# A four-image convolution, attention and top-k expert kernel: image 0's opening rewritten, and expert masks built on ScalarE

## The reference, cut to what matters

```python
# block 1, per image
x_ln = layernorm(x, ln_g, ln_b)
q = x_ln @ wq + bq                                   # read as an image of 128 channels
o = gelu(depthwise_conv_7x7_stride2(q_img) + dw_b)   # 8x8 positions
offsets = conv_1x1(o)
interp = grid_sample_bilinear_zeros(x, tanh(offsets) + refs)
k, v = interp @ wv + bv                              # 64 keys
att = softmax(qh @ kh.T) @ vh                        # 8 heads
z = att @ mo_w + mo_b + x
t = gelu(layernorm(z) @ mlp_w + mlp_b) + z
# block 2
t = t + landmark_attention(ln(t))                    # 4 best of 16 segments per head
# block 3
q = layernorm(ln(t) @ Wq.T + bq)                     # 8 heads
sc0, ix0 = top_k(l2norm(q[:half]) . l2norm(keys0), 16);  sc1, ix1 = the same for the other half
fs, pos = top_k(all sums sc0 + sc1, 16);  fi = ix0 + ix1 at pos
w = softmax(fs)
out = sum over the 16 of gelu(t . expert_down[fi]) * w * expert_up[fi]
t = t + out
```

## Time and profile before

| | us |
|---|---|
| median of 3 runs | 451.5 |
| lowest and highest | 449.02, 451.69 |
| the profiled execution, device time | 449.87 |
| its span, first to last instruction | 447.8 |
| mean granted TensorE clock | 0.701 |

### The profile page before, as it was taken

The page is one execution under the profiler, slowest core; times in us unless marked ns, Lnnn a source line. Parts: engine busy times, 40 slices in busy tenths (PEclk is TensorE's granted clock), DMA queues, the critical chain, the costliest instruction groups (busy, mean ns, idle before and its releaser), DMA issues.

```text
span 447.8 us, 7841 instructions
## 1 busy us (share of the span) xinstructions
PE 308.1 (69%) x2275; PEld 225.2 (50%) x2275; DVE 358.4 (80%) x2163; ACT 140.7 (31%) x324; POOL 217.9 (49%) x411
## 2 busy tenths in 40 slices
...
DMA packets 1634, 3.50 MB, mean 8 GB/s; under 512 B 180, under 2 KB 1205, under 8 KB 1592
## 3 DMA queue, kind: packets, MB, share of 16 engines
...
## 4 chain that ended last, share of the span: by engine, by line
DVE 55%; PE 23%; POOL 9%; issue 6%; ACT 6%; DMA 1%; DVEq 0%; ACTq 0%; POOLq 0%
PE bank L876 6%; DVE Sx L1363 5%; DVE i L1369 5%; DVE i L1370 5%; DVE cands L1419 4%; DVE onehot L494 4%; DVE vraw L1366 3%; DVE vraw L1360 3%; DVE segmax L1244 3%; DVE c L1416 3%; PE bank L540 2%; PE bank L550 2%; DVE masked L1426 2%; PE bank L783 2%; ACT hat L914 2%
## 5 line engine op out<-in xcount | busy, mean ns | idle before, releaser
L876 PEld LDWEIGHTS bank<-weights,onehot 108*128 108x128 f16 x1024 | 69.0, 178 | 3.1 <-DVE onehot L494 1.5
L876 PE MATMUL bank<-weights,onehot 108*128 108x16 f16 x1024 | 69.0, 216 | 1.9 <-DVE onehot L494 1.4
L1644 POOL TENSOR_TENSOR inv<-nrm,mhalf 128x16 f32<-128x16 f32 x8 | 23.4, 2925 | 35.8 <-DVE nrm L1376 35.8
L458 POOL TENSOR_TENSOR taps<-qpad,wa 128x128 f32<-128x128 f32 x96 | 36.0, 427 | 2.0 <-ACT qpad L929 1.9
L540 PE MATMUL bank<-wa,hat 128*128 128x128 f32 x24 | 6.7, 371 | 32.9 <-ACT hat L914 32.9
L1557 POOL TENSOR_TENSOR rstd<-veps,mhalf 128x2 f32<-128x2 f32 x16 | 11.7, 731 | 34.6 <-DVE veps L1166 34.3
L1370 DVE FIND_INDEX8 i<-vraw,Sx 128x8 uint16<-128x64 f32 x128 | 28.0, 219 | 0.0
L1369 DVE FIND_INDEX8 i<-vraw,S 128x8 uint16<-128x64 f32 x128 | 28.0, 218 | 0.0
L1363 DVE MATCH_REPLACE8 Sx<-vraw,S 128x64 f32<-128x64 f32 x128 | 25.1, 209 | 0.0
L803 PE MATMUL bank<-KB,qsT 128*128 128x256 f32 x64 | 24.9, 558 | 0.2 <-issue 0.2
L494 DVE TENSOR_SCALAR onehot<-eT 108x512 f16<-108x512 uint16 x84 | 24.4, 366 | 0.0
...
## 6 DMA issues: line engine op xcount, KB each, us to landing
...
bq_row<-rows_dram SPq DMA_DIRECT2D x1, 0.5 KB
...
```

Source lines behind the costliest of these rows:

```text
L458: ins = eng.tensor_tensor(tv[:, :, :, ky, kx:kx + n], q, dw[:, ky, kx:kx + n].unsqueeze(1).unsqueeze(1).broadcast_to([P, G8, G8, n]), ALU. ...
L876: last = mm(o[:, g * 16:g * 16 + 16], OHv[:, c * NT + t, g], Rv[:, c, t, g, s], start=(c == 0 and s == 0), stop=(c == NCH - 1 and s == 1))
L1644: g_.tensor_tensor(inv[:, n], nrm[:, n], mhalf[:, 0:2 * H], ALU.pow).then_inc(inv_ready, 1)
```

## The change

- Image 0's opening: the first 441 columns of `wa` (the query weights, gain and bias rows, vectors and tap weights) come in a DMA of their own. POOL's first memsets of `qpad`, `rts` and `bias` go to DVE. DVE writes `xln` itself (`H0`): `(x - mean) * gain`, then `* rstd`. The layer norm's bias goes through PE as two more products with `wq`.
- The convolution of image 0: 21 taps on DVE as running sums over four accumulators, 14 taps on ACT, 14 on POOL with one add, then four adds and a reduction of four on DVE.
- For image 0, DVE also writes `hat` of the other three layer norms (`H1`, `H2`, `H3`) and subtracts the maxima in `F5a`, so that ACT needs one exponential of 512 columns for each half.
- ScalarE's `TE` and `TG`: an exponential and a gelu of one element, placed to load the tables.
- Images 0, 1, 2: ACT builds `lom` (`N3c`) and four of the 32 one-hots (`N3e`), each as |value - x| for four values and one relu(1 - |...|). DVE's `N3b` has 24 masks left, and `R` is a stage of its own, `N3d`, behind `N3b`.
- `negmean` goes away: POOL multiplies the mean by `rstd` and -1 in two instructions.
- New orders and banks. There are 13 `W` (26 matmuls of filler) in place of 21.

Orders, cut to what the text speaks of (the rows for DVE have only the new stages beside the old order):

```diff
-    "tensor": A1a.0 A2d.0 A1b.0 W.0 W.1 A3a.0 A3b.0 A3c.0 A4.0 W.2 W.3 F5a.0 A1a.1 F5c.0 NS.0 F6a.0 F6b.0 W.4 W.5
-        F6c.0 F7a.0 F7b.0 F8a.0 A1b.1 F8b.0 F9b.0 A2d.1 F9a.0 F9c.0 A3a.1 A3b.1 W.6 A3c.1 A4.1 W.7 W.8 F8c.0
-        F9d.0 W.9 F10a.0 F10b.0 F11a.0 F11t.0 F5a.1 F11b.0
+    "tensor": A1a.0 A2d.0 W.0 W.1 W.2 W.3 A1b.0 W.4 A3a.0 A3b.0 A3c.0 A4.0 F5a.0 A1a.1 F5c.0 F6a.0 NS.0 F6b.0 F6c.0
+        F7a.0 F7b.0 W.5 A1b.1 W.6 F8a.0 F8b.0 F9b.0 A2d.1 F9a.0 F9c.0 A3a.1 A3b.1 A3c.1 A4.1 F8c.0 W.7 F9d.0
+        F10a.0 F10b.0 F11a.0 F5a.1 F11t.0 F11b.0
-        F10b.3 F11a.3 N6b.1 F11t.3 W.12 W.13 F11b.3 F11c.3 W.14 N3a.2 F12.3 N0a.3 N0h.3
+        N4.2 N6b.1 F11t.3 F11b.3 F11c.3 W.11 N3a.2 W.12 F12.3 N0a.3 N0h.3
...
-    "scalar": A0b.0 A1a.0 A2c.0 A2d.0 A3a.0
+    "scalar": A1a.0 A2a.0 TE.0 A2c.0 A2d.0 A1b.0 A3a.0
-        F11b.1 N3a.0 F5b.2 F12.1 N4.0 F5c.2 N0a.1 N0h.1 A0b.3 A1a.3 F6b.2 N0b.1
+        F11b.1 F5b.2 N3a.0 F12.1 N3c.0 F5c.2 N0a.1 N0h.1 A0b.3 N3e.0 F6b.2 N0b.1
-        F5b.3 N3a.1 F12.2 F5c.3 N0a.2 N0h.2 N4.1 F6b.3 N0b.2 N0c.2
+        F5b.3 N3a.1 F12.2 F5c.3 N0a.2 N0h.2 N3c.1 N0b.2 F6b.3 N3e.1 N0c.2
-        N3a.2 F12.3 N0a.3 N0h.3 N0b.3 N0c.3 N0d.3 N4.2 N0e.3
+        N3a.2 F12.3 N0a.3 N0h.3 N3c.2 N0b.3 N4.2 N0c.3 N0d.3 N3e.2 N0e.3
...
-    "vector": A0a.0 A2c.0 A3a.0 NB.0 A0a.1 F5a.0 NS.0 F6a.0
+    "vector": A0a.0 H0.0 A2c.0 A3a.0 NB.0 A0a.1 F5a.0 NSa.0 NSb.0 NSc.0 NSd.0 NSe.0 F6a.0 F6c.0 H1.0 F7b.0 H2.0
-        N3a.0 N3b.0 N0a.1
+        N3a.0 N3b.0 N3d.0 N0a.1
-        F6a.3 N0b.2 N3b.1 A3a.2 N1_0.2
+        F6a.3 N0b.2 N3b.1 N3d.1 A3a.2 N1_0.2
-        N0b.3 N3b.2 N0d.3
+        N0b.3 N3b.2 N3d.2 N0d.3
```

The code, cut:

```diff
             sp.dma_start(x_sb[:, 0, :, :], x_in[0]).then_inc(x_loaded[0], 16)
-            sp.dma_start(wa[:, :], wa_in).then_inc(wa_loaded, 16)
+            first = offA["ident"][0]
+            sp.dma_start(wa[:, 0:first], wa_in[:, 0:first]).then_inc(wa0_loaded, 16)
             sp.dma_start(bq_row[0:1, :], rows_in[0:1, 0:C]).then_inc(bq_loaded, 16)
+            sp.dma_start(wa[:, first:NA], wa_in[:, first:NA]).then_inc(wa_loaded, 16)
...
                 mm(o[:, 0:N], ones[0:1, :], bq_row[0:1, :].unsqueeze(1).broadcast_to([1, NT, C]), start=True, stop=False)
+                if b == 0:
+                    mm(o[:, 0:N], A("lnb"), A("wq").unsqueeze(1).broadcast_to([P, NT, C]), start=False, stop=False)
+                    oT = take("qT", b)
+                    mm(oT[:, 0:N], A("wq"), A("lnb").unsqueeze(1).broadcast_to([P, NT, C]), start=True, stop=False)
                 pe.wait_ge(xln_ready, b + 1)
...
+            def A2a(b):
+                dw = A("dw")
+                read_out(ac, "qimg", b)
+                for k in range(CONV_DVE, CONV_POOL * KS):
+                    last = fn(tap(k), window(k), ACT.Identity, scale=dw[:, k:k + 1])
+                last.then_inc(taps_act_ready, 1)
+                copy_qT(b)
...
+            def equal(dst, src, values):
+                n = len(values)
+                for k, value in enumerate(values):
+                    last = fn(away[0:KC, k, :], src, ACT.Abs, scale=-1.0, bias=A("iota")[0:KC, value:value + 1])
+                link(last)
+                return fn(dst, away[0:KC, 0:n, :], ACT.Relu, scale=-1.0, bias=ones[0:KC, 0:1])
+            def N3c(b):
...
+                equal(lom[0:KC, :, :], eT[0:KC, 1, :], list(range(LO))).then_inc(lom_ready, 1)
+            def N3e(b):
+                hi = range(ACT_HI)
+                ac.wait_ge(lom_ready, b + 1)
+                equal(OH[0:KC, :, :, 0:ACT_HI, :].rearrange("p n q v g -> p v (n q) g"), eT[0:KC, 2, :],
+                      [LO * h for h in hi]).then_inc(onehot_act_ready, 1)
...
-                v.tensor_scalar(negmean[:, k, :], mv[:, k, :, 0], -1.0, None, ALU.mult)
                 v.tensor_scalar(veps[:, k, :], mv[:, k, :, 1], LN_EPS, None, ALU.add).then_inc(var_ready[k], 1)
+            def hats(k, src, b):
+                dve.wait_ge(rstd_ready[k], b + 1)
+                for t in range(NT):
+                    last = v.tensor_scalar(hat[:, k, t, :], src[:, t, :], mv[:, k, t, 0:1], rstd[:, k, t:t + 1],
+                                           ALU.subtract, ALU.mult)
+                last.then_inc(hat_ready[k], 1)
...
-                    link(conv_rows(v, 0, CONV_DVE))
+                    for k in range(CONV_DVE):
+                        i = k % SUMS
+                        if k < SUMS:
+                            ins = v.tensor_scalar(tap(i), window(k), dw[:, k:k + 1], None, ALU.mult)
+                        else:
+                            dve.wait_ge(sums_ready, k - SUMS + 1)
+                            ins = v.scalar_tensor_tensor(tap(i), window(k), dw[:, k:k + 1], tap(i), ALU.mult, ALU.add)
+                        ins.then_inc(sums_ready, 1)
+                    dve.wait_ge(taps_act_ready, 1)
                 dve.wait_ge(taps_pool_ready, b + 1)
+                if b == 0:
+                    link(add_taps(v, 22, 32, 10))
+                    link(add_taps(v, 22, 27, 5))
+                    link(add_taps(v, 21, 24, 3))
+                    link(add_taps(v, 0, 21, 3))
...
+            def N3d(b):
+                if b == B - 1:
+                    return
+                dve.wait_ge(lom_ready, b + 1)
+                read_out(dve, "wT", b)
+                for lo in range(LO):
+                    last = v.tensor_tensor(R[0:KC, :, lo, :], W2[0:KC, :, :],
+                                           lom[0:KC, lo, :].unsqueeze(1).broadcast_to([KC, 2, NCH * N]), ALU.mult)
+                last.then_inc(R_ready, 1)
...
-                for hi in range(POOL_HI, HI):
+                for hi in range(POOL_HI + ACT_HI if b < B - 1 else POOL_HI, HI):
```

More of the change, by code:

```diff
@@ L50 @@
 HI = E // LO
-CONV_DVE = 4
+CONV_DVE = 21
+CONV_POOL = 5
+SUMS = 4
 FOLDED = 4
 POOL_HI = 4
+ACT_HI = 4
 FILL = 2
@@ L109 @@
 ORDERS = {
-    "tensor": """A1a.0 A2d.0 A1b.0 W.0 W.1 A3a.0 A3b.0 A3c.0 A4.0 W.2 W.3 F5a.0 A1a.1 F5c.0 NS.0 F6a.0 F6b.0 W.4 W.5
-        F6c.0 F7a.0 F7b.0 F8a.0 A1b.1 F8b.0 F9b.0 A2d.1 F9a.0 F9c.0 A3a.1 A3b.1 W.6 A3c.1 A4.1 W.7 W.8 F8c.0
[L112 to L121, removed]
```

241 lines of the change are left out of this document (170 added, 71 removed).

## The result

The changed kernel takes 457.73 us (median of 4 runs, 456.08 to 458.61) against 451.16 of the kernel before: ratio 1.0145, 95% interval 1.0117 to 1.0174. The forecast was 444.5. The profiled execution has a span of 456.4 us against 447.8. It is the longest of the four; in the profiles of experiments 4, 6 and 7, whose opening is the same to the instruction, the first MAX8 comes some 2 us sooner (108.9 to 109.3) than in it. The profile of the kernel before has such a spread too: in experiment 8, whose opening is that of before to the instruction, the first MAX8 comes at 102.58 and not at 105.38. Between the two late profiles the opening lost 5.65 us, between the early ones 6.3 to 6.8.

The account below looks back on a forecast made before the run. Image 0's chain of steps was taken to bound the first 100 us, DVE's list 100 to 400 us. Opening -9.0 and images 0 to 2 +2.1 gave -6.9: 443.0 profiled, 444.5 beside the median, range 434 to 452.

Parts of the forecast that it names:

- To the segment maxima: Image 0, `rec` to segment maxima: 18.1 us instead of 21.55, from layer norms, removed filler and reordered PE work.
- ACT's 0.88 "for DVE's 0.35": Image 0's next two layer norms: losing `shift` and moving `hat` from ACT to DVE saves 0.8 us each, -1.6.
- if POOL's folds of image 1 don't hold DVE: Condition on the -1.2 us from `F8b` following PE's transposed `tT` at once, on the way to image 0's segment maxima.
- Convolution: Image 0's convolution, taps to end: 7.1 us instead of 10.8, -3.7, bounds -5 to -1; DVE's taps at 0.2 each.
- Scores to rec: Image 0, first scores (`negM`) to `rec`: 13.4 us instead of 12.0, +1.4 for two more DVE subtractions.
- First layer norm: Image 0's start: taps begin at 8.35 us instead of 10.17, -1.8, bounds -3.3 to 0.
- Convolution to scores: Image 0, convolution's end to `negM`: +0.5 us on 12.15, the middle between filler costing time and raising PE's clock.
- To image 0's top keys: Image 0, segment maxima to first MAX8: -1.8 us, with one filler less before the bias transposes counted as -0.9.
- Masks: Images 0 to 2: emptied wait before `ssq` stays, `R` adds time; 0, +1.3 and +1.0; +2.1 us in all.
- The removed DVE work counts in full: Rival, images 0 to 2: masks, low digits and `negmean` all come off, -7.3 us instead of +2.1: 435; chance 0.19.
- ACT didn't become the bound: Rival at ACT's masks: groups taking 7 us delay `S` and `qsT`, +9.2 us: 454; sign turns near 6.2; chance 0.1.
- The opening gives half: Rival, image 0's opening: filler at low clock, taps at 0.34 us, gain only 4.8 us: 449; chance 0.13.

Follow-up runs that it names:

- experiment 4: Changed kernel with all masks, low digits and `R` back on DVE, ACT's copies for image 0 ahead of image 2's exponentials: ratio 1.0065 to the kernel before.
- experiment 6: Changed kernel with ACT's copies for image 0's masks ahead of image 2's exponentials: ratio 1.0123 to the kernel before.
- experiment 7: Experiment 6 with `lom` and `R` back on DVE ahead of `ssq`, ACT keeping its four one-hots: ratio 1.0001 to the kernel before.
- experiment 8: Kernel before, with only DVE's `R` of images 0 to 2 moved behind its one-hots: ratio 1.0067 to the kernel before.
- experiment 1: Changed kernel with POOL waiting for `hat` before its folds of image 1's taps: ratio 1.0014 to the kernel before.
- experiment 2: Changed kernel with image 0's hats of layer norms 1 and 2 back on ACT, folds not held back: ratio 1.0038 to the kernel before.
- experiment 9: On experiment 1: DVE's centring behind `rec`, POOL's root between image 1's tap halves, 1.0021; then also POOL's next root ahead of both folds, 0.9955.

## Why the prediction was wrong

The step that failed is one and the same in three places: DVE's instructions were priced at the duration they have alone, where POOL works beside them. By the figures below that is some 9 of the 14.6 us (4.75, 2.3 and 2.0), an estimate.

- **To the segment maxima (+6.0, the largest).** The step that failed is ACT's 0.88 "for DVE's 0.35". The 0.35 stands in no row, and it is about what one hat takes with POOL idle. Measured: 0.60 for the two alone, 3.69 and 2.89 beside POOL's folds; experiments 1 and 2 show that it is DVE against POOL, and mending it brought back 4.75 us of this step. The prediction had named the condition ("if POOL's folds of image 1 don't hold DVE") and gave it no price and no chance. The trace of before couldn't show a DVE hat beside a fold, since its hats were on ACT. The Trainium skill ("SBUF — State Buffer", Who interferes with whom) states it: a VectorE `tensor_scalar` in a 2-port mode and a GpSimd instruction exclude each other, and the second stands for the whole instruction. The hat (3.69 us) and POOL's root (6.22) agree with it, in both directions; that the hat was in such a mode no row shows. By that sentence, with the fold's 3.4 us from the trace, the first hat would have been put at 3 us more, an estimate.
- **Convolution (+2.1).** The same step, and the bounds had held it. DVE's taps at 0.2 us each are right for DVE alone: eleven of them took 0.20. The ten beside POOL took 0.42, and that makes 6.5 us for 21 and not 4.2. The row that the upper bound came from, 0.34 for a tap, had POOL's taps beside it too. POOL (4.2 for 4.3), ACT (3.6 for 3.0) and the adds with the reduction (2.7 for 2.8) are right or harmless. No experiment took POOL's taps away from here, so this is read from the trace alone.
- **Scores to rec (+2.0).** The two subtractions cost what was said. The rest is DVE beside POOL's taps again: one instruction takes 2.19 us for 1.02 before, another 1.61 for 0.68. POOL's taps ran beside both in either kernel; why they hold DVE up more here I can't say. It cost less than it seems, since POOL's list came later (experiment 9).
- **First layer norm (+1.9).** The table loads were weighed behind the taps, where they are hidden, and not in front of them: removing `A0b.0` left `qpad` as ACT's first function, 1.3 us. PE's three products start at 4.30 for 3.9 and take 3.0 us for 2.6. No gain was left of 1.8.
- **Convolution to scores (+0.2): right in size, in part by luck.** Both halves of the working happened: PE rose to its high clock in the filler, and the filler cost its own time. But the step took 12.8 us in this profile and 11.2 in those of experiments 4, 6 and 7; before it took 12.15, and 9.7 in experiment 8. A difference of +0.5 can't be read from such profiles. One reading was off: PE's matmuls of 22 to 35 us were slow to about 31 only (two of 256 columns at 34.06 took 0.69 us, not 1.22).
- **To image 0's top keys (+2.2).** The removed fillers were booked as gain. PE ran at half clock through 84 to 92 us where it had been at full. What moves this isn't settled: `W.9` back in brought 1.5 us in one run and nothing with the hats mended.
- **Masks (+0.9 of 3.0): right in mechanism and place; the size is in part luck.** "The wait stays, is now empty, and R comes on top" is what experiments 7 and 8 show. In image 0 the exponentials' turn cost 1.7 where the prediction had it balanced against the saved work, in image 1 it was 2.1 for 1.3, in image 2 nothing for 1.0, and the tail gave 0.8 back. In image 2 DVE before had a second wait, 1.65 us in front of the other half's `ssq`, of which 0.48 is left; the prediction didn't have it. From `ssq` to the masks that gives 0.7 back and from `eT` to `ssq` it takes 0.4 less, and the two take up the 1.2 that `R` adds over the masks saved.
- **Rivals.** "The removed DVE work counts in full" is out by experiments 7 and 8. ACT didn't become the bound: 4.6 us for a group of four, against 6.2 for the turn. "The opening gives half" had taps at 0.34 us, near the 0.31 that came, and missed the hats. The slower case that happened, an engine's instruction stretched by a neighbour, was no rival on my list.
